# The last expert's output in two PSUM banks, its row tiles weighted and scattered one by one

## What is computed

```
gates = softmax(x2d @ wg); idx = argmax(gates)          # 2048 tokens, E = 8
mask  = one_hot(idx) * (place of the token in its expert < C)   # C = 256
h  = relu(einsum('ecm,emh->ech', di, w1))               # per expert 256 x 1024
eo = einsum('ech,ehm->ecm', h, w2)                      # per expert 256 x 256
x  = x + tanh(g_ffn[3]) * einsum('sfc,fcm->sm', combine, eo)
```

## Time and profile before

| | us |
|---|---|
| median of 3 runs (lowest, highest) | 938.06 (937.97, 940.6) |
| profiled execution: its own time | 940.78 |
| profiled execution: span, first to last instruction | 939.0 |
| TensorE busy | 844.2 (90%) |
| VectorE busy | 454.4 (48%) |
| ScalarE busy | 327.5 (35%) |
| GpSimd busy | 207.0 (22%) |
| mean granted TensorE clock | 0.961 |

### The profile page before, as it was taken

How to read it: one execution, slowest core, us unless ns; L and a number is a source line. 1 busy time by engine, 2 the same in 40 slices (tenths; PEclk the granted TensorE clock), 3 DMA queues, 4 the chain that set the end, 5 groups by cost and what they waited for, 6 DMA issues and landing times. The chain is left out here.

```text
span 939.0 us, 15120 instructions
## 1 busy us (share of the span) xinstructions
PE 844.2 (90%) x5806; PEld 652.3 (69%) x5806; DVE 454.4 (48%) x1240; ACT 327.5 (35%) x629; POOL 207.0 (22%) x226
## 2 busy tenths in 40 slices
PE   7897999999999997889998999988998896399996
PEld 5775655777888875666766676655776675388885
DVE  2685544420132316576667667756887686000000
ACT  2332222113322223554545455555443431022121
POOL 1114500011424311000001001214663115212212
PEclk9896999999999999999999999999999995599999
DMA  6030910005646446000000000000000012336451
GB/s 226 23 125 34 335 52 23 23 7 197 218 141 202 113 131 240 1 2 1 1 1 1 2 1 2 2 1 1 1 2 1 23 43 82 124 102 201 144 155 20
DMA packets 33873, 70.58 MB, mean 75 GB/s; under 512 B 9218, under 2 KB 23946, under 8 KB 28939
## 3 DMA queue, kind: packets, MB, share of 16 engines
q1 hardware_dynamic: 26937, 59.92, 18.0%
q0 software_dynamic: 6144, 8.31, 4.6%
q10 hardware_dynamic: 722, 1.39, 0.4%
HBM read 54.98 MB, written 14.80 MB: 74 GB/s over the span
## 5 line engine op out<-in xcount | busy, mean ns | idle before, releaser
L591 PE MATMUL banks<-arena 32*120 32x256 f32 (+6 forms) x1808 | 164.1, 378 | 15.5 <-DVE small L1876 12.7
L1219 ACT ACTIVATE arena<-banks 128x512 f32<-128x512 f32 (+4 forms) x185 | 107.0, 597 | 166.0 <-PE banks L1017 33.4
L591 PEld LDWEIGHTS banks<-arena 32*120 32x120 f32 (+5 forms) x1808 | 102.5, 163 | 51.1 <-issue 32.6
L591 PE MATMUL banks<-ffw,arena 128*128 128x256 f32 (+2 forms) x640 | 117.8, 340 | 1.4 <-DVE x L1957 1.4
L591 PE MATMUL banks<-arena,ew 128*128 128x256 f32 x512 | 115.4, 384 | 1.4 <-ACT arena L1219 1.4
L591 PE MATMUL banks<-ew,arena 128*128 128x256 f32 x512 | 113.2, 379 | 0.0
L591 PEld LDWEIGHTS banks<-arena,ew 128*128 128x128 f32 x512 | 98.6, 193 | 15.7 <-ACT arena L1219 2.0
L591 PEld LDWEIGHTS banks<-ew,arena 128*128 128x128 f32 x512 | 96.2, 190 | 12.5
L591 PEld LDWEIGHTS banks<-ffw,arena 128*128 128x128 f16 (+1 forms) x640 | 85.2, 136 | 26.4 <-issue 4.2
L1876 DVE TENSOR_REDUCE small<-banks 128x16 f32<-128x1920 f32 x32 | 69.0, 2157 | 20.8 <-PE banks L591 20.7
L1397 ACT ACTIVATE arena<-banks,mcol 120x2048 f32<-120x2048 f32 x32 | 63.1, 1971 | 19.0 <-PE banks L591 19.0
(11 more groups left out here) (239 smaller groups left out, 1246.6 us busy)
## 6 DMA issues: line engine op xcount, KB each, us to landing
ew<-in_w SPq DMA_DIRECT2D x32, 1024.0 KB
xrow<-arena SPq DMA_DIRECT2D x1, 2064.0 KB, 22.0
arena<-xrow SPq DMA_DIRECT2D x8, 258.0 KB, 4.5
zrow<-arena SPq DMA_DIRECT2D x8, 256.0 KB, 2.2
ffw<-in_shared SPq DMA_DIRECT2D x2, 1024.0 KB, 6.5
acc<-x SPq DMA_DIRECT2D x4, 512.0 KB
ffw<-in_tern SPq DMA_DIRECT2D x2, 1024.0 KB, 8.7
out<-x SPq DMA_DIRECT2D x8, 256.0 KB, 2.0
```

The lines of the kernel that those rows point to most:

```text
L591: return pe.matmul(o, l, r, start=a, stop=b)
L1219: return nc.scalar.activation(o, i_, ACT.Copy)
```

## The change

For the last expert alone (`n` = 7), the product of tile 1 goes to bank 6 and not to the second half of bank 5. TensorE signals a new semaphore `half` behind tile 0's eight instructions, and `y_ps` behind tile 1's as before. VectorE waits for each tile's own signal, multiplies it, and signals `y_sb` behind each. GpSimd waits for the scatter of expert 6 first, then for each tile's `y_sb`, and issues that tile's indirect DMA. Experts 0 to 6 stay as they are. The number and the shape of products, multiplications and DMAs stay the same.

```diff
-        ex = sems("experts", "w0 w1 gather0 gather1 gather2 rows0 rows blank xT_ps xT_sb h_ps h_sb y_ps y_sb o0 o1 acc")
+        ex = sems("experts", "w0 w1 gather0 gather1 gather2 rows0 rows blank xT_ps xT_sb h_ps h_sb y_ps y_sb half o0 o1 acc")
...
-            for e in range(E):
+            for e in range(E - 1):
                 g.wait_ge(ex["y_sb"], E + e + 1)
                 scatter(e, rows_out, lambda e, j: G3.bitcast(I32)[:, e, j, D:D + 1], E + e, bounds_check=T - 1, oob_is_err=False)
+            g.wait_ge(ex[f"o{(E - 2) % 2}"], 32 * E)
+            for j in range(TB):
+                g.wait_ge(ex["y_sb"], 2 * E + j)
+                g.indirect_dma_start(rows_out, bass.IndirectOffsetOnAxis(ap=G3.bitcast(I32)[:, E - 1, j, D:D + 1], axis=0),
+                                     eout[:, (E - 1) % 2, j, :], None, compute_op=ALU.add, bounds_check=T - 1,
+                                     oob_is_err=False).then_inc(ex[f"o{(E - 1) % 2}"], 16)
             phase_end(g, 2)
...
+                    split = i * 2 + u == 2 * E - 1
                     for t in range(TB):
+                        bank = psum[6] if split and t else psum[4 + u]
                         for k in range(MC):
                             if t == 0:
                                 pe.wait_ge(q["h_sb"], i * 2 * MC + u * MC + k + 1)
-                            m = mm(psum[4 + u][:, t * D:(t + 1) * D], heT[:, u, k, t * P:(t + 1) * P], w[:, k, :],
+                            m = mm(bank[:, t * D:(t + 1) * D], heT[:, u, k, t * P:(t + 1) * P], w[:, k, :],
                                    k == 0, k == MC - 1)
+                        if split and t == 0:
+                            m.then_inc(q["half"], 1)
                     m.then_inc(q["y_ps"], 1)
...
-                    v.wait_ge(q["y_ps"], E + n + 1)
+                    if n < E - 1:
+                        v.wait_ge(q["y_ps"], E + n + 1)
                     if n >= 2:
                         v.wait_ge(q[f"o{u}"], 16 * E + 32 * (n // 2))
                     for t in range(TB):
-                        m = V.tensor_scalar(eout[:, u, t, :], psum[4 + u][:, t * D:(t + 1) * D], G3[:, n, t, D + 1:XROW],
+                        if n == E - 1:
+                            v.wait_ge(q["y_ps" if t else "half"], 2 * E if t else 1)
+                        bank = psum[6] if n == E - 1 and t else psum[4 + u]
+                        m = V.tensor_scalar(eout[:, u, t, :], bank[:, t * D:(t + 1) * D], G3[:, n, t, D + 1:XROW],
                                             None, ALU.mult)
-                    m.then_inc(q["y_sb"], 1)
+                        if t or n == E - 1:
+                            m.then_inc(q["y_sb"], 1)
```

## The result

The changed kernel took 936.47 us (median of 20 runs, 934.01 to 943.34), the kernel before, measured beside it, 938.48 (20 runs, 936.09 to 940.82). The ratio is 0.9978 with an interval of 0.9967 to 0.9988: faster by 0.22%, 2.0 us. The profiled execution of the changed kernel has a span of 935.56 us and a time of 937.32.

The account below looks back on a forecast made before the run. TensorE bounds the kernel to 929.97 us, then a 9.03 us tail without it. Tile 1's earlier weighting (0.40) and no wait for scatter 0 (1.85) take 2.25 us off the median 938.06: 935.81; range 934.6 to 938.4.

Parts of the forecast that it names:

- (a): TensorE's last product: second bank and extra signal cost 0 to 0.38 us; taken as 0.
- (b): Tile 0 of the last product: ready 3.45 us earlier, weighted and scattered while TensorE still works on tile 1.
- (c): Tile 1 after the product's end: weighting starts 0.40 us earlier, no wait for scatter 0 saves 1.85; 2.25 us together.
- The price of the wait: Gap from tile 1's weighting on VectorE to its scatter on GpSimd: between 0.27 and 0.75 us; 0.75 taken.
- Rival B: Tile 1's wait is met at the scatter, not the MOVE: 2.76 us saved in all, 935.30 us; chance 0.17.
- (d): After scatter 1: GpSimd's closing DRAIN follows the last landing and moves with it; span 936.75 us, 2.25 less.
- rival A: GpSimd's closing DRAIN costs 6.53 us from its own start: only 0.9 us saved, 937.2 us; chance 0.07.
- The sum: Saving in the tail after the last product: 0.40 + 1.85 = 2.25 us.
- Rival C: VectorE cannot use tile 0's signal until the whole product is done: 937.66 us; chance 0.04.
- Rival D: Tile 1's weighting on VectorE and scatter 0's preparation on GpSimd block each other, losing up to 1.55 us: 937.4; chance 0.03.
- Rival E: TensorE's clock falls to 1.2 GHz over the last expert's 64 records, costing 13.81 us: 949.6 us; chance 0.04.
- Rival F: Rest of the program differs by the runs' spread, 2.63 us: 938.4 (chance 0.06) or 933.2 (chance 0.07).

Follow-up runs that it names:

- the load beside scatter 1: Changed kernel plus one unused 1 MB weight load on SyncE's queue, started when the last product is done; timed once, 938.14 us.
- the first experiment: Changed kernel, but VectorE waits for the whole product before weighting tile 0; ratio 0.999 to the kernel before, tail 8.79 us.
- the one with the register ahead: Changed kernel with the bound of the last expert's scatters put in a register once, ahead of the waits; ratio 0.9978 to the kernel before.

## Why the prediction was right

935.8 us was predicted, 0.24% under the kernel before; 936.47 was measured, 0.22% under. The mechanism is shown by the tail. That the medians agree as closely as that has some luck in it: measured again, the same kernel was 0.16% under. Taken off the median of the 20 runs of before instead of the 3, my 2.25 would have given 936.23.

(a) TensorE unchanged: right, 20.74 us for 96 records in both, at a clock of 1.00. No run keeps both tiles in one bank and signals each by itself, so what the second bank is worth stays open.

(b) Tile 0 under the second half: right in kind; the weighting came 3.36 us ahead of the product's end where I had 3.43, and the scatter ended 0.48 ahead where I had 0.62. Two wait records of their own, which I did not foresee, are the difference (0.07 us each), and they cost nothing, as they lay under the product.

(c) Tile 1: scatter 1 at 1.29 behind the product's end, forecast 1.28. The price of the wait was the upper bound, 0.75, since the wait stood on the MOVE. Rival B named the right mechanism and its price (0.50 measured against my 0.51) but the changed kernel doesn't have it.

(d) The end: DRAIN moves with the landing. This was argued from two DRAINs of different length, and the DRAIN of 5.25 us refuted rival A at once; the load beside scatter 1 pulled landing and preparation apart, whose distance hardly varies in the other traces of this tail.

The sum: 2.25 forecast, 2.20 measured. 0.04 went to the landing.

Rival C did not occur (tile 0 is weighted 3.36 us early); undone by hand (the first experiment) the early weighting costs 1.94 us. Rival D had no occasion: tile 1's weighting began 0.51 us after scatter 0's preparation ended, and took 0.48 as always. Rival E: the clock stayed 1.00 to the end of the product, as 20.74 us for 96 records says. Rival A is refuted under (d). Rival F is real, in both directions, and was the weak point of a forecast for the time: what the runs differ by is as large as the effect.

## What to carry to other kernels

When the last product of a kernel ends, everything behind it is serial: cut that chain by having all but the last piece of output through every engine of it before the product ends, and check each link, because one late link gives nearly all of the saving back (1.9 of 2.2 us here). Then look at what the last wait stands on (here a MOVE that could go ahead of it, 0.5 us) and at who really waits for a DMA's landing (here a DRAIN, 1.3 us behind it). The same edit at an earlier stage was worth nothing here, where its consumer is led by something else: read the first use of the data, not the wait for the DMA.

## What the runs showed of the hardware that was not expected

GpSimd's DRAIN behind its own indirect DMAs waits for their data: it ended 1.33 to 1.35 us behind the landing in every trace here, with lengths from 5.2 to 7.5 us, and the load beside it showed that it follows the landing.

The start of the kernel is what varies from run to run. The first mixture's last product ended at 335.30 in the profile of before, 334.00 in that of the changed kernel and 330.96 in the one with the register ahead; from there to the last product's end all three took 594.4 to 594.7 us, and the other seven profiles 593.8 (the one with the load) to 594.75. The first 100 us differ in the granted clock. Stretches of the kernel before (busy us by engine, then the granted clock, DMA share, GB/s):

```profile
0.00:30.00 30.00, 22.56 (x121) 18.15 (x122) 8.64 (x31) 8.62 (x22) 3.39 (x13) 1.00 0.53 177
30.00:60.00 30.00, 27.62 (x166) 22.86 (x165) 21.81 (x83) 10.57 (x35) 6.01 (x8) 0.89 0.08 27
60.00:100.00 40.00, 32.46 (x143) 22.20 (x142) 25.05 (x79) 12.13 (x30) 18.65 (x20) 0.79 0.39 129
```

and of the kernel with the register ahead:

```profile
0.00:30.00 30.00, 22.13 (x128) 17.81 (x129) 9.93 (x35) 9.39 (x26) 3.39 (x13) 0.94 0.53 177
30.00:60.00 30.00, 27.18 (x187) 22.37 (x186) 24.35 (x92) 11.92 (x38) 6.01 (x8) 1.00 0.22 73
60.00:100.00 40.00, 32.98 (x125) 20.79 (x125) 23.66 (x76) 11.33 (x26) 22.56 (x27) 0.79 0.39 135
```

The stretch from 30 to 60 us ran at a mean of 0.89 in the one and of 1.00 in the other, that is, with and without time at 1.2 GHz, and TensorE had 166 and 187 records in it; no edit of this study touches instructions there.

The 1.00 and 0.94 of the first stretch can't be compared. The trace has no record of the clock before 19.6 us in the kernel before and before 11.8 in the other, and the view counts what has no record as full. The products tell more. Records of one form, in the kernel before (L591) and in the one with the register ahead (L598), in the view by source line of 12 to 15 us:

```profile
L591 PE MATMUL banks<-cols,arena x14: 352/352/352, 11.7 to 14.4; 128*128 128x1 f32 x14
```
```profile
L598 PE MATMUL banks<-cols,arena x12: 250/250/250, 11.9 to 13.1; 128*128 128x1 f32 x12
```

So TensorE was slower in the kernel before already there. Read by the same instruction of ScalarE in both, the lead of the second kernel is 1.44 us at its 21st (27.99 and 26.55 us) and 4.29 at its 41st (46.65 and 42.36), of 4.34 at the end of the first mixture. What sets off the low stretches was not tried.
